# Two layers of cross attention on one core: queries of two units projected together in every second slot

## The chip, the cores and the metric

The kernel runs on one core of a Trainium2 chip. The metric is device time in microseconds (us) of one execution. The core has four compute engines that run their own instruction streams and meet only at semaphores: PE (TensorE, matrix products into the accumulation banks), ACT (ScalarE), DVE (VectorE) and POOL (GpSimd). SP issues the DMA transfers in this kernel, one after another, and each issue takes SP's time.

## The reference

There are 32 batches of x [112, 512], a context [375, 512] and an additive mask [112, 375], which is zero in these inputs. Two layers follow each other, each of this form (32 query heads of 16, 8 key and value heads, groups of 4):

```python
q = x @ Wq + bq;  k = ctx @ Wk + bk;  v = ctx @ Wv + bv
scores = einsum('bkgld,bksd->bkgls', q, k) * scale + mask
attn = softmax(scores);  out = einsum('bkgls,bksd->bkgld', attn, v)
x = layernorm(out @ Wo + bo + x) * gamma + beta
```

All of it is float32 on the outside. The context is the same for both layers.

## The kernel before, in words

A unit is one batch in one layer: 64 units, in two parities p = 0 and 1 (batch 2n + p is unit n of parity p). The program is a row of slots, (0, i), (1, i), (0, i + 1) and so on, and each engine's stream is written out by hand slot by slot in `run`, with a loop over i in the middle of each layer. In slot (p, i) five units are worked on (`units`, L57): `main` has its scores, exps and weighted values made; `ahead`, of the other parity o, gets its values projected and its row maxima; `post`, of parity o, gets its second half of weighted values and its output projection; `proj`, of parity p, gets keys and queries projected; `stored`, of parity p, gets its residual, layer norm and store.

A slot has 12 pieces. In each, PE makes two score products `sc` (L746, 448 columns), and around them stands other work. `maximum` (L754) makes a pair of products `ms` whose row maxima DVE takes; 16 pairs a slot, spread over the pieces by `PAIRS_AT`. `values` (L767) multiplies probabilities and values into the bank `pv`, 12 products for half a unit. `max_columns` (L788) turns the maxima, as negated bf16 parts, into `job`; ACT casts them to `mT`, and a DMA puts them as rows into `qs`, so that the score product subtracts the maximum. `project_values` (L795), `project_keys` (L806), `project_outputs` (L817), `transpose_rows` (L830, layer 0 only) and `project_queries` (L840) are float32 products.

There are eight banks: two for `sc`, four for `ms`, one `pv` (values, keys, turned rows) and one `job` (projected values, queries, outputs, turned maxima). Each user of `job` first waits until the last one has been emptied (`take_job_bank`, L732).

Queries: PE fills `job` with four heads of 112 columns (L846, 16 products), ACT adds the bias and scales into `qf` (L565), and the float32 is split into three bf16 parts `qp` (ACT L570 and L579, POOL L483 and L491). Keys go the same way into `kp`. SP then copies the parts into stacked operands `qs` and `ks` by small transfers (`stack_terms`, L301): 6 terms for each of q and k and for each half of the heads, 24 a slot. The first half (h = 0) is issued at the end of a slot, the second at the start of the next. SP's other transfers in a slot are two rows of `mT` (L310), four of `oraw` (L315, L316), the mask (L270), the context (L265), the turned x (`xT`, L278), x (L288), the result y (L294) and in layer 0 its turned form (L299). Scores cannot start before the `mT` row has landed (L750), nor the maxima of a half before its stack has (L756).

Of the kernel before, what the change touches and what calls it, by code (L numbers as in the profile page):

```python
# [8 lines left out]
ALU = mybir.AluOpType  # L9
ACT = mybir.ActivationFunctionType  # L10
# [10 lines left out]
KC = 3  # L21
# [79 lines left out]
def cross_attention_two_layers(nc, xT_d, x_d, ctxT_d, mask_d, mflat_d, W, out):  # L101
# [4 lines left out]
    with ExitStack() as ctx:  # L106
# [40 lines left out]
        xT = two(sb, "xT", [P, DC, S])  # L147
# [3 lines left out]
        qf = sb("qf", [P, GL])  # L151
# [57 lines left out]
        q_ps = two(sem, "q_ps")  # L209
# [4 lines left out]
        q_evac = two(sem, "q_evac")  # L214
# [39 lines left out]
        def _(sp):  # L254
# [17 lines left out]
            def load_xT(p, n, layer):  # L272
                b, before = batch(p, n, layer), count(n)
                turned = count(16 * (n - PER) + 16) if layer == 1 else 0
                need(sp, q_ps[p], before)
                need(sp, yT_out[p], turned)
                src = xT_d if layer == 0 else yT_d
                sp.dma_start(xT[p][:, :, :].rearrange("p a b -> p (a b)"), src[b]).then_inc(xT_in[p], 16)  # L278
# [39 lines left out]
            def slot(p, i, has, lay):  # L318
# [19 lines left out]
                if m_ok:  # L338
                    max_rows(p, 1, count(2 * main + 2))
                if s_ok:  # L340
                    store_y(p, stored, lay[4])
                if more and not (isinstance(ahead, int) and ahead + 1 == 0):
                    after = lay[3] if not isinstance(ahead, int) else 0 if ahead + 1 < PER else 1
                    load_ctx(o, ahead + 1, after)
                    load_xT(o, ahead + 1, after)
                if m_ok:
                    load_x(p, main, lay[0])
                if j_ok:
                    sp.wait_ge(k_p3[p], keys)
                    stack_terms(p, 0, ks[p], kp[p], 1)  # L350
                    sp.wait_ge(q_p1[p], queries)
                    stack_terms(p, 0, qs[p], qp, 0, of=(0,))
                if m_ok:
# [46 lines left out]
            load_xT(0, 0, 0)  # L400
            for n in range(BLOADS):
# [3 lines left out]
            load_xT(1, 0, 0)  # L405
# [7 lines left out]
        def _(pool):  # L413
# [15 lines left out]
            def slot(p, i, has, lay):  # L429
# [30 lines left out]
                if m_ok:  # L460
                    max_parts(p, 1, main, (p, 2 * main + 1))
                if s_ok:
                    pool.wait_ge(ln[p], 3 * (stored + 1))
                    nc.gpsimd.tensor_tensor(rstd[:, :], veps[:, :], neghalf[:, :], ALU.pow).then_inc(rs_ready[p], 1)
                if p_ok:
                    pool.wait_ge(x_in[o], 16 * (post + 1))
                    if s_ok:
                        pool.wait_ge(o_evac[p], stored + 1)
                    nc.gpsimd.tensor_tensor(res[:, :], xin[o][:, :], bo[lay[2]][:, :], ALU.add).then_inc(res_ready[o], 1)
                if j_ok:  # L470
# [4 lines left out]
                if p_ok:  # L475
                    weighted(0)
                if a_ok:
                    max_parts(o, 0, ahead, (p, 2 * main + 2) if m_ok else None)
                if j_ok:
                    for h in range(2):  # L480
                        cols = slice(GL // 2 * h, GL // 2 * (h + 1))
                        pool.wait_ge(q_p1[p], 2 * proj + h + 1)
                        nc.gpsimd.tensor_tensor(qr[:, cols], qf[:, cols], qp[:, 0, cols], ALU.subtract)\  # L483
                          .then_inc(q_r[p], 1)
                if p_ok:
                    weighted(1)
                if j_ok:
                    for h in range(2):
# [3 lines left out]
                          .then_inc(q_p3[p], 1)  # L492

# [4 lines left out]
        def _(act):  # L498
            def slot(p, i, has, lay):
# [31 lines left out]

                for k in range(PIECES):
# [3 lines left out]
                    if k == 4 and j_ok:  # L536
                        act.wait_ge(k_ps[p], proj + 1)
                        if a_ok:
                            act.wait_ge(k_r[o], ahead + 1)
                        if m_ok:  # L540
                            act.wait_ge(stack[p][0], 16 * NSTACK * (main + 1))
                            act.wait_ge(stack[p][1], 16 * NSTACK * (main + 1))
                        nc.scalar.activation(kf[:, :], pv[:, 0:S2], ACT.Identity, bias=bk[lay[3]][:, 0:1])\
                          .then_inc(k_evac[p], 1)
                        act.wait_ge(k_evac[p], proj + 1)
                        nc.scalar.copy(kp[p][:, 0, :], kf[:, :]).then_inc(k_p1[p], 1)  # L546
                    if k == 3 and m_ok:
                        m_out(p, 1, main, (p, main + 1))
                    if k == 5 and j_ok:
                        act.wait_ge(k_r[p], proj + 1)  # L550
                        nc.scalar.copy(kp[p][:, 1, :], kr[:, :]).then_inc(k_p2[p], 1)
                    if k == 6 and s_ok and lay[4] == 0:
                        act.wait_ge(t_ps[p], stored + 1)
                        if not isinstance(stored, int) or 2 * stored + p > 0:
                            need(act, yT_out[o], 16 * (stored + p))
# [418 lines left out]
```

## Time and profile before

| what | value |
|---|---|
| time, median of 3 runs | 1839.72 us (1838.92 to 1845.19) |
| the profiled execution | 1841.82 us |
| its span, first to last instruction | 1839.7 us |
| mean granted TensorE clock | 0.986 |
| busy share of PE, DVE, ACT, POOL | 97%, 74%, 59%, 31% |
| chain that ended last, PE's share | 88% |

Spans and starts are microseconds from the first instruction. A line of the timeline is a run of equal instructions. An f32 product stands as two records, so 8 products are x16. The ends of PE records are modelled and overlap the next record's start, so a distance from start to start tells PE's time better than the busy time. A granted clock of 1.00 is the 2.4 GHz level.

### The profile page before, as it was taken

How to read it: one execution, taken by the hardware profiler on the slowest of the kernel's cores; microseconds unless marked ns; L12 is line 12 of the kernel's file. 1: busy time of each engine (PE TensorE's matmuls, PEld its weight loads, DVE VectorE, ACT ScalarE, POOL GpSimd, SP SyncE). 2: the span in 40 equal slices, each digit the busy share in tenths (PEclk: the TensorE clock that was granted, in tenths of full speed). 3: DMA queues.
4: the chain of work that ended last, by engine and by line, in shares of the span. 5: the costliest groups of instructions: out<-in, count | busy, mean ns of one | idle time of the engine just before them, and what ended most of it. 6: DMA issues, size and time to landing. Idle time of an engine off the chain costs nothing.

```text
span 1839.7 us, 37410 instructions
## 1 busy us (share of the span) xinstructions
PE 1778.8 (97%) x11521; PEld 1148.1 (62%) x11521; DVE 1369.8 (74%) x1808; ACT 1079.1 (59%) x2530; POOL 573.1 (31%) x1165
## 2 busy tenths in 40 slices
PE   4899899999999999999999999999999999999996
PEld 3566566666666666666666666666666666666652
DVE  6577677777777777777777777777787777777784
ACT  1465556656656656656656656656655656656653
POOL 1232223323323323323323323323323333333321
PEclk8899999999999999999999999999999999999998
DMA  9235434434434434434434434434434434443421
GB/s 287 88 124 171 139 115 143 132 116 142 133 116 142 132 118 142 132 117 142 133 120 142 127 111 131 128 107 134 130 109 132 128 114 128 128 126 116 126 85 42
DMA packets 200894, 235.92 MB, mean 128 GB/s; under 512 B 41706, under 2 KB 176100, under 8 KB 199812
## 3 DMA queue, kind: packets, MB, share of 16 engines
q1 hardware_dynamic: 200836, 235.19, 41.6%
q8 instruction: 31, 0.51, 0.1%
q14 instruction: 27, 0.22, 0.0%
HBM read 101.39 MB, written 22.02 MB: 67 GB/s over the span
## 4 chain that ended last, share of the span: by engine, by line
PE 88%; SPq 5%; DMA 2%; issue 2%; ACT 1%; POOL 1%; DVE 0%; ACTq 0%; POOLq 0%; DVEq 0%
PE ms L763 17%; PE pv L782 16%; PE sc L746 14%; PE job L824 12%; PE job L846 11%; PE job L800 9%; PE pv L812 9%; SPq L305 4%; DMA qs<-qp 1%; PE pv L837 1%; DMA qs<-mT 1%; PE job L791 0%; DMA bq<-in_bq 0%; POOL kp L474 0%; POOL kr L472 0%
## 5 line engine op out<-in xcount | busy, mean ns | idle before, releaser
L632 DVE TENSOR_REDUCE mx<-ms 112x2 f32<-112x750 f32 x1024 | 933.4, 933 | 414.7 <-PE ms L763 402.8
L516 ACT ACTIVATE probs<-sc 125x448 f32<-125x448 f32 x1536 | 751.9, 542 | 345.3 <-PE sc L746 338.1
L763 PE MATMUL ms<-ks,qs 96*112 96x375 bf16 x2048 | 500.7, 326 | 14.1 <-DMA qs<-qp 11.8
L746 PE MATMUL sc<-qs,ks 99*125 99x448 bf16 x1536 | 422.2, 355 | 13.6 <-DMA qs<-mT 11.2
L763 PEld LDWEIGHTS ms<-ks,qs 96*112 96x112 bf16 x2048 | 252.9, 130 | 230.4 <-issue 116.4
L782 PE MATMUL pv<-probs,vs 125*32 125x448 f32 x3072 | 319.1, 549 | 0.0
L746 PEld LDWEIGHTS sc<-qs,ks 99*125 99x125 bf16 x1536 | 198.5, 137 | 129.7 <-ACT probs L516 74.7
L824 PE MATMUL job<-wo,on 128*112 128x512 f32 x512 | 268.6, 606 | 7.3 <-POOL on L458 5.7
L846 PE MATMUL job<-xT,wq 128*128 128x112 f32 x2048 | 248.8, 275 | 0.0
L846 PEld LDWEIGHTS job<-xT,wq 128*128 128x128 f32 x2048 | 244.2, 192 | 3.4 <-issue 0.3
L472 POOL TENSOR_TENSOR kr<-kf,kp 128x375 f32<-128x375 f32 x64 | 57.8, 903 | 537.4 <-ACT kp L546 537.4
L647 DVE RECIPROCAL orec<-osum 128x112 f32<-128x112 f32 x256 | 214.9, 841 | 10.3 <-DMA osum<-oraw 10.3
L812 PE MATMUL pv<-ctxT,wk 128*128 128x375 f32 x512 | 184.9, 483 | 10.4 <-DMA bq<-in_bq 10.4
L800 PE MATMUL job<-wv,ctxT 128*125 128x128 f32 x1536 | 190.8, 274 | 0.0
L782 PEld LDWEIGHTS pv<-probs,vs 125*32 125x32 f32 x3072 | 87.3, 110 | 164.2 <-issue 163.4
L800 PEld LDWEIGHTS job<-wv,ctxT 128*125 128x125 f32 x1536 | 186.5, 189 | 4.1
L524 ACT COPY oraw<-pv 128x448 f32<-128x448 f32 x128 | 68.1, 532 | 171.7 <-PE pv L782 171.7
L812 PEld LDWEIGHTS pv<-ctxT,wk 128*128 128x128 f32 x512 | 96.0, 191 | 49.7 <-issue 12.1
L565 ACT ACTIVATE qf<-job,bqs 128x112 f32<-128x112 f32 x256 | 69.8, 355 | 88.0 <-PE job L846 88.0
L444 POOL TENSOR_TENSOR mwide<-mx,zero 112x16 bf16<-112x16 f32 x128 | 27.6, 215 | 278.8 <-DVE mx L632 271.2
L491 POOL TENSOR_TENSOR qp<-qr,qp 128x224 bf16<-128x224 f32 x128 | 75.4, 610 | 104.7 <-ACT qp L579 104.7
L824 PEld LDWEIGHTS job<-wo,on 128*112 128x112 f32 x512 | 82.6, 177 | 37.4 <-issue 17.7
(54 smaller groups left out, 1000.4 us busy)
## 6 DMA issues: line engine op xcount, KB each, us to landing
ctxT<-in_ctxT SPq DMA_DIRECT2D x64, 750.0 KB, 5.9
qs<-qp SPq DMA_DIRECT2D x768, 56.0 KB, 2.4
ks<-kp SPq DMA_DIRECT2D x768, 46.9 KB, 2.6
osum<-oraw SPq DMA_DIRECT2D x128, 112.0 KB, 2.6
oc<-oraw SPq DMA_DIRECT2D x128, 112.0 KB, 2.6
mask<-in_mask SPq DMA_DIRECT2D x64, 164.1 KB, 2.3
xT<-in_xT SPq DMA_DIRECT2D x32, 224.0 KB, 6.6
xin<-in_x SPq DMA_DIRECT2D x32, 224.0 KB, 6.7
```

What stands on the lines that cost most here:

```text
L305: sp.dma_start(dst[HD * t:HD * t + HD, 4 * h:4 * h + 4, :].rearrange("d g n -> d (g n)"), src[64 * h:64 * h + 64, parts[which], :]).then_i ...
L491: nc.gpsimd.tensor_tensor(qp[:, 2, cols], qr[:, cols], qp[:, 1, cols], ALU.subtract)\
L516: nc.scalar.activation(probs[0:KCS, k, j, :], sc[j][0:KCS, 0:GL], ACT.Exp)\
L632: nc.vector.tensor_reduce(mx[o][:, 2 * j:2 * j + 2], ms[j % 2][0:S, :, 0:S2], AX_X, ALU.max)\
L647: nc.vector.reciprocal(orec[:, S * n:S * n + S], osum[:, S * n:S * n + S])\
L746: last = nc.tensor.matmul(sc[j][0:KCS, 0:GL], ks[p][0:KM, g, rows], qs[p][0:KM, g, :], start=True, stop=not masked)
L763: last = nc.tensor.matmul(ms[j % 2][0:S, n, 0:S2], qs[o][0:KT, g, S * c:S * c + S], ks[o][0:KT, g, :], start=True, stop=True)
L782: last = nc.tensor.matmul(pv[32 * j:32 * j + 32, 0:GL], vs[u][:, chunk, 4 * h + j, :, :].rearrange("s d two -> s (d two)"), probs[0:KCS, H ...
L800: last = nc.tensor.matmul(job[0:KCS, P * c:P * c + P], ctxT[o][:, t, KCS * c:KCS * c + KCS], wv[lay[1]][:, t, :], start=(t == 0), stop=(t ...
L812: last = nc.tensor.matmul(pv[:, 0:S2], wk[lay[3]][:, t, :], ctxT[p][:, t, :], start=(t == 0), stop=(t == DC - 1))
L824: last = nc.tensor.matmul(job[0:S, 0:D], on[:, S * c:S * c + S], wo[lay[2]][:, c, :], start=(c == 0), stop=(c == NG - 1))
L846: last = nc.tensor.matmul(job[:, S * c:S * c + S], wq[lay[3]][:, t, c, :], xT[p][:, t, :], start=(t == 0), stop=(t == DC - 1))
```

## The change

The queries of both units of one index (parities 0 and 1) are projected in slot (0, i), each product over 224 columns (`xT` holds both units side by side), and slot (1, i) has no query products. The four heads no longer fit in `job` at once: heads 0 and 1 fill its 448 columns, ACT moves them to `qf` (now for two units), then come heads 2 and 3. Slot (1, i) still splits its own unit's queries out of `qf`.

The output projection of the post unit of parity 1 is divided: heads 0 and 1 stay in slot (0, i), at pieces 10 and 11, and heads 2 and 3 come in pieces 0 and 1 of slot (1, i) (`LATE_HEADS_AT`). The places of all other PE steps, of the ACT, DVE and POOL steps that answer them, and of SP's transfers are now written per parity.

```diff
-PAIRS_AT = [2, 2, 1, 2, 0, 1, 1, 1, 2, 2, 1, 1]
+PAIRS_AT = [[1, 1, 1, 1, 1, 1, 1, 2, 1, 2, 2, 2], [1, 1, 1, 1, 2, 1, 1, 1, 2, 2, 2, 1]]
+LATE_HEADS_AT = [{}, {0: (2,), 1: (3,)}]
+HEADS_AT = [{10: (0,), 11: (1,)}, {8: (0,), 9: (1,), 10: (2,), 11: (3,)}]
+KEYS_AT = [{2: (0,), 3: (1, 2), 4: (3,)}, {2: (0, 1), 3: (2, 3)}]
+VALUES_AT = [{1: (0, 1), 2: (2,)}, {4: (0, 1), 5: (2,)}]
+QUERIES_AT = [{4: (0,), 5: (1,), 6: (2,), 7: (3,)}, {}]
+COLUMNS_AT = [(9, 3), (7, 2)]
+TURNED_AT = [6, 6]
+FIRST_HALF_AT = [8, 7]
+QUERY_PARTS_AT = [7, 4]
+RESIDUAL_AT = [0, 1]
+ROWS_AT = [4, 3]
...
-        xT = two(sb, "xT", [P, DC, S])
+        xT = sb("xT", [P, DC, PAR, S])
-        qf = sb("qf", [P, GL])
+        qf = sb("qf", [P, PAR, GL])
...
+                if p == 1 and (not isinstance(proj, int) or 0 < proj + 1 < UNITS):
+                    after = lay[3] if not isinstance(proj, int) else 0 if proj + 1 < PER else 1
+                    for u in range(PAR):
+                        load_xT(u, proj + 1, after)
...
+                def q_out(heads):
+                    act.wait_ge(q_ps, 2 * proj + heads[-1] // 2 + 1)
+                    if heads[0] == 0:
+                        for u in range(PAR):
+                            need(act, q_r[u], 2 * proj)
+                    for c in heads:
+                        nc.scalar.activation(qf[:, :, S * c:S * c + S],
+                                             job[:, PAR * S * (c % 2):PAR * S * (c % 2 + 1)].rearrange("p (u l) -> p u l", u=PAR),
+                                             ACT.Identity, bias=bqs[lay[3]][:, c:c + 1], scale=SCALE).then_inc(q_evac, 1)
...
                     def project_queries(heads):
+                        if heads[0] % 2 == 0:
+                            take_job_bank()
                         if 0 in heads:
-                            take_job_bank()
-                            pe.wait_ge(xT_in[p], 16 * (proj + 1))
+                            for u in range(PAR):
+                                pe.wait_ge(xT_in[u], 16 * (proj + 1))
                         for c in heads:
                             for t in range(DC):
-                                last = nc.tensor.matmul(job[:, S * c:S * c + S], wq[lay[3]][:, t, c, :], xT[p][:, t, :],
+                                last = nc.tensor.matmul(job[:, PAR * S * (c % 2):PAR * S * (c % 2 + 1)], wq[lay[3]][:, t, c, :],
+                                                        xT[:, t, :, :].rearrange("p u l -> p (u l)"),
                                                         start=(t == 0), stop=(t == DC - 1))
-                        if NG - 1 in heads:
-                            last.then_inc(q_ps[p], 1)
-                            job_free[0] = (q_evac[p], NG * (proj + 1))
+                        if heads[-1] % 2 == 1:
+                            last.then_inc(q_ps, 1)
+                            job_free[0] = (q_evac, NG * proj + heads[-1] + 1)
...
-                        next_maximum()
+                        if k > 0 or p == 0:
+                            next_maximum()
+                        if k in LATE_HEADS_AT[p] and s_ok:
+                            project_outputs(p, stored, lay[4], LATE_HEADS_AT[p][k])
```

PE, from piece 5 of a slot on, before (any parity; `sc` scores, `ms` a maxima pair, `job<-xT,wq` queries, `pv<-ident,y` turned rows, `pv<-probs,vs` weighted values):

```order
L763 MATMUL ms<-ks,qs 112x375 x2
L846 MATMUL job<-xT,wq 128x112 x8
L746 MATMUL sc<-qs,ks 125x448 x2
L763 MATMUL ms<-ks,qs 112x375 x2
L837 MATMUL pv<-ident,y 128x112 x4
L846 MATMUL job<-xT,wq 128x112 x8
L746 MATMUL sc<-qs,ks 125x448 x2
L763 MATMUL ms<-ks,qs 112x375 x2
L782 MATMUL pv<-probs,vs 32x448 x12
```

The same engine in the slot of parity 0 now, from piece 4 on:

```order
L921 MATMUL job<-xT,wq 128x224 x4
L818 MATMUL sc<-qs,ks 125x448 x2
L835 MATMUL ms<-ks,qs 112x375 x2
L921 MATMUL job<-xT,wq 128x224 x4
L818 MATMUL sc<-qs,ks 125x448 x2
L835 MATMUL ms<-ks,qs 112x375 x2
L909 MATMUL pv<-ident,y 128x112 x4
L921 MATMUL job<-xT,wq 128x224 x4
L818 MATMUL sc<-qs,ks 125x448 x2
L835 MATMUL ms<-ks,qs 112x375 x2
L921 MATMUL job<-xT,wq 128x224 x4
```

Two groups of two heads have become four of one head with twice the columns, one piece earlier, and the third needs the bank of the first two.

PE behind the first-half values, before (`job<-negident,mwide` turned maxima, `job<-wo,on` an output head):

```order
L782 MATMUL pv<-probs,vs 32x448 x12
L791 MATMUL job<-negident,mwide 128x112
L746 MATMUL sc<-qs,ks 125x448 x2
L763 MATMUL ms<-ks,qs 112x375 x2
L824 MATMUL job<-wo,on 112x512
L763 MATMUL ms<-ks,qs 112x375 x2
```

The same place in the slot of parity 0 now:

```order
L854 MATMUL pv<-probs,vs 32x448 x12
L818 MATMUL sc<-qs,ks 125x448 x2
L835 MATMUL ms<-ks,qs 112x375 x2
L863 MATMUL job<-negident,mwide 128x112
L835 MATMUL ms<-ks,qs 112x375 x2
L818 MATMUL sc<-qs,ks 125x448 x2
L835 MATMUL ms<-ks,qs 112x375 x2
L896 MATMUL job<-wo,on 112x512
```

The turned maxima stand behind a scores pair, and the first output head comes one piece later.

SP from the loads of x to the end of a slot, before (`ks<-kp` and `qs<-qp` stacked parts, `qs<-mT` the maxima rows):

```order
L265 DMA ctxT<-in_ctxT 128x1500
L278 DMA xT<-in_xT 128x448
L288 DMA xin<-in_x 112x512
L305 DMA ks<-kp 16x4x375 x6
L305 DMA qs<-qp 16x4x448 x3
L315 DMA osum<-oraw 64x448
L316 DMA oc<-oraw 64x448
L310 DMA qs<-mT 3x16x112
L305 DMA qs<-qp 16x4x448 x3
```

The same stretch in the slot of parity 1 now, in layer 1:

```order
L296 DMA xT<-yT_mid 128x4x112 x2
L306 DMA xin<-in_x 112x512
L323 DMA ks<-kp 16x4x375 x6
L283 DMA ctxT<-in_ctxT 128x1500
L323 DMA qs<-qp 16x4x448 x5
L328 DMA qs<-mT 3x16x112
L333 DMA osum<-oraw 64x448
L334 DMA oc<-oraw 64x448
L323 DMA qs<-qp 16x4x448
```

The context load stands behind the keys, both `xT` loads ahead of them, and only the last query part is left at the end.

## Rows read from the trace of the kernel before

**Rows 1.** The page: busy time and share of each engine.

```profile
PE 1778.8 (97%) x11521; PEld 1148.1 (62%) x11521; DVE 1369.8 (74%) x1808; ACT 1079.1 (59%) x2530; POOL 573.1 (31%) x1165
```

**Rows 2.** Table by stage: window, length, busy PE, PEld, DVE, ACT, POOL, clock, DMA.

```profile
550.00:715.00 165.00, 164.79 (x1091) 107.63 (x1090) 125.36 (x169) 101.69 (x239) 53.36 (x108) 1.00 0.42 131
1210.00:1375.00 165.00, 164.80 (x1078) 106.94 (x1077) 127.66 (x171) 100.48 (x237) 53.41 (x108) 1.00 0.40 123
```

**Rows 3.** Timeline of PE, layer 0: start, length, line, operation.

```profile
806.18 2.46 PE L782 MATMUL pv<-probs,vs 125*32 125x448 f32 x24
...
820.04 1.91 PE L800 MATMUL job<-wv,ctxT 128*125 128x128 f32 x16
821.79 0.48 PE L763 MATMUL ms<-ks,qs 96*112 96x375 bf16 x2
...
825.77 2.06 PE L812 MATMUL pv<-ctxT,wk 128*128 128x375 f32 x6
827.67 0.54 PE L746 MATMUL sc<-qs,ks 99*125 99x448 bf16 x2
828.05 0.48 PE L763 MATMUL ms<-ks,qs 96*112 96x375 bf16 x2
828.37 1.94 PE L846 MATMUL job<-xT,wq 128*128 128x112 f32 x16
830.14 0.55 PE L746 MATMUL sc<-qs,ks 99*125 99x448 bf16 x2
...
833.01 0.54 PE L746 MATMUL sc<-qs,ks 99*125 99x448 bf16 x2
...
833.81 2.46 PE L782 MATMUL pv<-probs,vs 125*32 125x448 f32 x24
836.20 0.22 PE L791 MATMUL job<-negident,mwide 112*128 112x112 bf16 x1
...
836.65 0.48 PE L763 MATMUL ms<-ks,qs 96*112 96x375 bf16 x2
837.19 1.11 PE L824 MATMUL job<-wo,on 128*112 128x512 f32 x2
838.14 0.49 PE L763 MATMUL ms<-ks,qs 96*112 96x375 bf16 x2
...
841.04 1.02 PE L824 MATMUL job<-wo,on 128*112 128x512 f32 x2
841.90 0.54 PE L746 MATMUL sc<-qs,ks 99*125 99x448 bf16 x2
```

**Rows 4.** Timeline of PE, layer 1: the second-half values of two slots.

```profile
1229.59 2.46 PE L782 MATMUL pv<-probs,vs 125*32 125x448 f32 x24
...
1256.81 2.46 PE L782 MATMUL pv<-probs,vs 125*32 125x448 f32 x24
```

**Rows 5.** Timeline of ACT, the same slot of layer 0.

```profile
833.42 1.09 ACT L565 ACTIVATE qf<-job,bqs 128x112 f32<-128x112 f32 x4 [1.39 <-PE job L846]
...
836.47 0.53 ACT L524 COPY oraw<-pv 128x448 f32<-128x448 f32 x1 [0.53 <-PE pv L782]
836.89 0.24 ACT L530 CAST mT<-job 48x112 bf16<-48x112 f32 x1
837.04 0.97 ACT L516 ACTIVATE probs<-sc 125x448 f32<-125x448 f32 x2
```

**Rows 6.** Timeline of DVE, the same slot.

```profile
838.66 3.66 DVE L632 TENSOR_REDUCE mx<-ms 112x2 f32<-112x750 f32 x4 [0.55 <-PE ms L763]
```

**Rows 7.** Timeline of SP's issues, the same slot.

```profile
831.51 3.78 SPq L305 DMA_DIRECT2D ks<-kp  x6
...
838.52 0.81 SPq L310 DMA_DIRECT2D qs<-mT  x1
839.38 1.90 SPq L305 DMA_DIRECT2D qs<-qp  x3
```

**Rows 8.** The chain that ended last, near the start: a transfer from issue to landing.

```profile
56.09 2.30 DMA qs<-qp
```

More of the change, by code:

```diff
@@ L49 @@
 PAIRS = NH // 2
-PAIRS_AT = [2, 2, 1, 2, 0, 1, 1, 1, 2, 2, 1, 1]
-PAIR0 = [sum(PAIRS_AT[:k]) for k in range(PIECES + 1)]
+PAIRS_AT = [[1, 1, 1, 1, 1, 1, 1, 2, 1, 2, 2, 2], [1, 1, 1, 1, 2, 1, 1, 1, 2, 2, 2, 1]]
+PAIR0 = [[sum(at[:k]) for k in range(PIECES + 1)] for at in PAIRS_AT]
 HH = NH // 2
 NSTACK = 2 * NT
-assert KCS * KC == S2 and PAIR0[-1] == PAIRS and KM <= P and PAIR0[7] >= PAIRS // 2
+LATE_HEADS_AT = [{}, {0: (2,), 1: (3,)}]
[9 more added lines that the diff above has]
+ROWS_AT = [4, 3]
+RECIPROCALS_AT = [4, 4]
+KEYS_END = [max(at) for at in KEYS_AT]
+VALUES_END = [max(at) for at in VALUES_AT]
+assert KCS * KC == S2 and KM <= P and all(at[-1] == PAIRS and at[n[0]] >= PAIRS // 2 for at, n in zip(PAIR0, COLUMNS_AT))
 def units(p, i):
@@ L208, in cross_attention_two_layers @@
         v_ps = two(sem, "v_ps")
-        q_ps = two(sem, "q_ps")
+        q_ps = sem("q_ps")
         o_ps = two(sem, "o_ps")
@@ L213, in cross_attention_two_layers @@
         k_evac = two(sem, "k_evac")
-        q_evac = two(sem, "q_evac")
+        q_evac = sem("q_evac")
         k_p1 = two(sem, "k_p1")
@@ L350, in slot @@
                     stack_terms(p, 0, ks[p], kp[p], 1)
+                if more and p == 1 and not (isinstance(ahead, int) and ahead + 1 == 0):
+                    load_ctx(o, ahead + 1, lay[3] if not isinstance(ahead, int) else 0 if ahead + 1 < PER else 1)
+                if j_ok:
                     sp.wait_ge(q_p1[p], queries)
                     stack_terms(p, 0, qs[p], qp, 0, of=(0,))
+                    if p == 1:
+                        sp.wait_ge(q_p2[p], queries)
+                        stack_terms(p, 0, qs[p], qp, 0, of=(1,))
+                if a_ok and p == 1:
+                    max_rows(o, 0, count(2 * ahead + 1))
                 if m_ok:
@@ L400, in _ @@
             load_xT(0, 0, 0)
+            load_xT(1, 0, 0)
             for n in range(BLOADS):
@@ L535, in slot @@
                         pv_out(o, 1, post, post + o)
[L536 to L549, printed above, removed]
+                    if k == KEYS_END[p] + 1 and j_ok:
                         act.wait_ge(k_r[p], proj + 1)
                         nc.scalar.copy(kp[p][:, 1, :], kr[:, :]).then_inc(k_p2[p], 1)
[L552 to L555, printed above, removed]
-                        nc.scalar.copy(yT[:, :, :].rearrange("p a b -> p (a b)"), pv[:, 0:GL])\
-                          .then_inc(yT_ready[p], 1)
-                    if k == 6 and j_ok:
-                        act.wait_ge(q_ps[p], proj + 1)
+                    if k == COLUMNS_AT[p][1] and m_ok:
+                        m_out(p, 1, main, (p, main + 1))
+                    if k == KEYS_END[p] and j_ok:
+                        k_out()
+                    if k == TURNED_AT[p] and s_ok and lay[4] == 0:
+                        rows_out()
+                    if k in QUERIES_AT[p] and QUERIES_AT[p][k][-1] % 2 == 1 and j_ok:
+                        q_out((QUERIES_AT[p][k][-1] - 1, QUERIES_AT[p][k][-1]))
+                    if k == QUERY_PARTS_AT[p] and j_ok:
                         if a_ok:
```

189 lines of the change are left out of this document (109 added, 80 removed).

## The prediction

> **What bounds the kernel now.** I read the page's busy shares, then a table by stage, then the PE timeline of one slot, then ACT, DVE and SP beside it. PE is busy for 97% of the span, DVE for 74% [rows 1]. In the steady stretches of both layers PE is busy for 164.8 of 165 us at a granted clock of 1.00 (the 2.4 GHz level) [rows 2], so a saving counts only if it shortens PE's stream or its waits. The profiler spreads busy time over short waits, so I take start-to-start distances. From the second `pv` group of one slot to that of the next it is 27.63 us in layer 0 (806.18 to 833.81 [rows 3]) and 27.22 in layer 1 [rows 4]. A pair of slots is thus 55.26 and 54.44 us. The profiled execution took 1841.82 us for a span of 1839.7; the median shown is 1839.72, so a change of the span carries over one to one.
>
> **Pitches.** All from [rows 3]. An f32 product is two records. 16 records of 112 columns (L846) take 830.14 − 828.37 = 1.77 us, 0.1106 each. 16 of 128 columns (L800) take 1.75, 0.1094 each. Six of 375 (L812) take 1.90, 0.3167 each. Two of 512 (L824) take 0.86, 0.430 each. So 112 columns cost no less than 128: below that width something other than columns sets the pace, the 128-column weight load. A scores pair is 0.38 and a maxima pair 0.32.
>
> **Query products.** Per pair of slots 64 records of 112 columns become 32 of 224. The nearest rows bound a record of 224 between 0.109 (128 columns) and 0.317 (375). The line through them gives 0.1094 + 96 × 0.00084 = 0.190, and at 512 it gives 0.432 against the measured 0.430, so I hold 0.190 to within 0.005. Removed 64 × 0.1106 = 7.08, added 32 × 0.190 = 6.08: −1.00 us per pair. At the bounds it would be −3.6 or +3.1, which I leave out of the range because of the fit at 512.
>
> A sentence by itself: the Trainium skill (TensorE: Matmul & The Clock Gate, "Back-to-back issue gap") gives a sustained spacing of 81 ns at 128 columns and 131 at 512, so wide products would be nearly free, and by an estimate from that the pair would save some 4 us. Here a bf16 product of 375 columns has half of 0.32, 160 ns, and the f32 row grows linearly with columns, so the trace disagrees and decides.
>
> **The first query evacuation.** Two units do not fit in one bank: heads 0 and 1 fill `job` (448 columns), and heads 2 and 3 must wait until ACT has emptied it (`take_job_bank` on `q_evac`). Before, all four heads had their own columns and no wait. After a query group ends (833.01, the next scores) `qf` starts 0.41 us later [rows 3, 5]. Four of 112 columns take 1.09, 0.27 each, and two of 448 take 0.97, 0.49 each [rows 5]; 224 columns lie at 0.34, so two need about 0.75 with the tail. The bank is free 0.41 + 0.75 + 0.04 = 1.20 us after head 1 ends. Between head 1 and head 2 stand a scores pair and a maxima pair, 0.70, and in layer 0 the turning of rows, 0.39. PE waits 0.50 in layer 1 and 0.11 in layer 0, and pays a weight load that is not hidden: the first output product after such a wait takes 0.95 against 0.86 [rows 3], +0.09. Together +0.59 and +0.20. Ends: 0, if ACT is quicker by all of it, and 1.20, if nothing covers it.
>
> A rule speaks against this edit, in a sentence by itself: the Trainium skill (Perfetto Trace Analysis, "Matmuls") says that independent groups should rotate through PSUM banks so that the evacuation of one overlaps the next. The trace agrees where it can: the output product at 837.19 starts just as the `mT` cast ends (836.89 + 0.24) [rows 3, 5].
>
> **After the first-half values.** In the slot of parity 0, `values` moves from piece 7 to 8 and `max_columns` to piece 9, behind the scores. ACT's `oraw` starts 0.27 after `pv` ends (836.20 to 836.47), the next operation 0.42 later, and an exp takes 0.54, a pair 0.97 [rows 5]. So the first exp of piece 9 ends 1.23 after `pv`, the second 1.67. PE reaches the scores of piece 10 after 0.38 + 0.32 + 0.06 + 0.32 = 1.08, must wait to 1.29 for the first bank and to 1.73 for the second, and is then 0.46 late. In return the first output product has no wait any more (before: 837.19 − 836.65 − 0.32 = 0.22, and the 0.09): −0.31. Ends for the +0.46: 0 and 0.7.
>
> **Parity 1.** Slot 1 loses all queries and gets the last two output heads, laid out 25.4 us in layer 1 (25.8 in layer 0); slot 0 becomes 28.8. Its first maxima pair comes only after `values`, 3.7 us into the slot, which leaves 21.7 us. DVE is busy 125.36 of 165 us, that is 21.0 per slot of 27.63 [rows 2]. Of this two maxima of 0.92 (four in 3.66 [rows 6]) may end in the next slot, so DVE keeps up, with 2 to 3 us in hand at the end and, where maxima come in twos in pieces 8 to 10, a few tenths. POOL's split of the first eight maxima ends about when `pv` does. I take +0.10 for all of it; ends 0 and 0.6.
>
> **SP's queue.** A stack transfer costs SP 0.63 (six in 3.78), an `mT` row 0.81 [rows 7], and a landing comes 2.30 after the issue, 2.9 from its start [rows 8]. Moved past in slot 1: both `xT` loads ahead of the keys, the `ctxT` load behind them, the middle query part and `mT` ahead of the outputs. The keys' last part is there 831.51 − 827.67 = 3.84 after their product [rows 3, 7]; that product ends 9.6 us into slot 1, so keys start at 13.5. Behind them 6 + 5 transfers, one load, one `mT` and two outputs end at 22.9, and the last query part lands at 25.8. PE wants it for the first maxima of slot 0, at 25.4 + 0.38. That cover is nearly nothing in layer 1, 0.5 in layer 0. In slot 0 `mT` starts at about 25.5 and lands near 28, with 0.8 to spare. Nothing added to the sum here, up to +1 per pair in the range.
>
> **The sum.** Layer 1: −1.00 − 0.31 + 0.59 + 0.46 + 0.10 = −0.16 per pair. Layer 0: −0.55. With 16 pairs of layer 0 and 15 of layer 1: −8.8 − 2.4 = −11.2 us. At the start the second slot projects keys ahead of values (2.6 us of PE earlier, 24 records of 0.109) and no queries, while the first slot has twice the query work behind SP's keys: −1.5 (−3 to +2). At the end the last slot of parity 0 sheds two output products of 0.86 while the next has room on PE: −1. Together −13.7: a span of 1826.0, and a median of 1826.0 us.
>
> **The rivals.**
> 1. No new waits: ACT empties the bank in time, or PE's waits only replace slack. Then the 1.00 stays whole: −31 − 2.5 = −33.5, 1806 us (with the freed output wait of 0.31 as well it could be 1797). For it: the 1.00 is PE work that disappears whatever the queues do. Against it: the latencies of [rows 5].
> 2. The waits eat it all: the bank wait of layer 1 in both layers (+0.39 × 16 = 6) and DVE or POOL late at parity 1 (+0.3 × 31 = 9): 1841 us, no change.
> 3. Slower: SP's queue decides. The last query part has no cover at the start of slot 0. Each 0.1 us by which the keys' parts or one of SP's own waits come later goes into PE's wait before the first maxima of slot 0. From 0.45 us per pair on the gain is gone; at 0.9 us it is +28 − 13.7: 1854 us. For it: SP issues 9.4 us without a pause behind the keys. Against it: the slot of parity 1 has slack before the keys' parts are ready.
> 4. The change does not do what it says: the 224 columns cost as much as two products of 112 (0.221). Then the 1.00 is gone: +31, 1857 us. Against it stands the line through three widths.
>
> **Chances.** The forecast 0.42 (1814 to 1836), rival 1 0.26, rival 2 0.17, rival 3 0.12, rival 4 0.03. Range 1804 to 1844: it leaves out the far end of rival 1 and most of rivals 3 and 4. A difference under 0.5% (9.2 us) is what a measurement of this kernel cannot tell from none. Faster by more than that (below 1830.5): 0.75 of the forecast's case and all of rival 1, 0.58. Within: 0.27. Slower: rivals 3 and 4, 0.15.
>
> **What would show it.** Right: query groups of 8 records at 1.52 us; a gap of 1.2 us between the end of head 1 and the weight load of head 2; scores of piece 10 that wait for exp behind `oraw`; slots of about 28.8 and 25.5 us. Wrong: PE waiting for `qs<-qp` at the start of parity 0 (rival 3), maxima waiting for DVE in pieces 8 to 11 of parity 1 (rival 2), or no wait ahead of head 2 (rival 1).

## The result: 0.23% faster, less than half of the forecast

| | before | after |
|---|---|---|
| time, median of 20 runs each | 1842.12 us (1836.52 to 1845.5) | 1837.86 us (1834.49 to 1841.65) |
| ratio of times, 95% interval | | 0.9977 (0.9969 to 0.9985) |
| span of the profiled execution | 1839.7 us | 1833.1 us |
| mean granted clock | 0.986 | 0.986 |

The gain is 4.3 us by the medians, where the prediction said 13.7. The time lies inside the range (1804 to 1844), but the gain is nearer to rival 2 ("the waits eat it all", 1841) than to the forecast. The prediction held that a difference under 0.5% cannot be told from none; with 20 executions on each side it can, and the interval leaves out 1. One execution of e9 (2280 us, granted clock 0.75) and one of e12 (1884 us, 0.94) further down ran at a lowered clock and stand in no time or ratio.

The page of the changed kernel answers to [rows 1]:

```profile
PE 1772.7 (97%) x10497; PEld 1105.6 (60%) x10497; DVE 1356.2 (74%) x1808; ACT 1049.3 (57%) x2402; POOL 589.4 (32%) x1165
```

PE has 1024 records fewer: 2048 of 112 columns became 1024 of 224. PE's busy time falls by only 6.1 us. The table by stage, the view of [rows 2], gives for a window in each layer (length, busy PE, PEld, DVE, ACT, POOL, clock, DMA):

```profile
465.00:630.00 165.00, 164.64 (x1001) 105.05 (x1000) 125.14 (x169) 99.34 (x228) 55.07 (x108) 1.00 0.44 132
...
1185.00:1350.00 165.00, 163.56 (x980) 101.59 (x972) 124.95 (x168) 96.95 (x222) 55.29 (x109) 1.00 0.42 123
```

PE is still the engine that is never free and the granted clock is the same 1.00, so the answer is in the stream of PE. The measure used from here on is the length of a **pair of slots**, from one second-half `pv` group to the one four groups later. It repeats to 0.02 us through most of a layer, and the tables give that value. A few pairs are longer, by up to 1.4 us, and in both kernels the two that start near 155 and 170 us are longer by 9 to 10 us: there SP issues the loads of layer 1's weights, and PE waits once for the maxima row (`qs<-mT`), 7.97 us before and 6.39 after. The time of a single execution scatters by some 4 us.

| | layer 0 | layer 1 |
|---|---|---|
| pair before (forecast took 55.26 and 54.44) | 55.30 | 54.50 |
| pair after | 54.83 | 54.83 |
| difference measured | −0.47 | +0.33 |
| difference forecast | −0.55 | −0.16 |

With 16 and 15 pairs this is −7.5 + 5.0 = −2.5 us. The start brought −3.0 (the first `pv` group of the steady stretch starts at 129.44 instead of 132.43), the longer pairs, the seam of the layers and the end the other −1.1 of the 6.6 by which the span fell. Not all of the −3.0 need belong to the change: the mean granted clock from 60 us to that group was 0.96 before and 1.00 after, and in the experiments e5 and e4, which leave the start nearly as it is, the same group starts at 127.68 and 131.67. The pairs do not hang on this. Layer 0 became faster and layer 1 slower.

**PE's timeline after, layer 1, slot of parity 0** (start, length, line, operation, records; in brackets the idle time that the profile sees before it). It answers to [rows 3]:

```profile
1228.36 1.68 PE L921 MATMUL job<-xT,wq 128*128 128x224 f32 x8
1229.87 0.54 PE L818 MATMUL sc<-qs,ks 99*125 99x448 bf16 x2
...
1232.47 0.48 PE L835 MATMUL ms<-ks,qs 96*112 96x375 bf16 x2
1233.12 1.78 PE L921 MATMUL job<-xT,wq 128*128 128x224 f32 x8 [0.17 <-ACT qf L614]
1234.74 0.54 PE L818 MATMUL sc<-qs,ks 99*125 99x448 bf16 x2
...
1238.07 2.46 PE L854 MATMUL pv<-probs,vs 125*32 125x448 f32 x24
1240.46 0.59 PE L818 MATMUL sc<-qs,ks 99*125 99x448 bf16 x2
...
1241.27 0.48 PE L835 MATMUL ms<-ks,qs 96*112 96x375 bf16 x2
1241.63 0.84 PE L818 MATMUL sc<-qs,ks 99*125 99x448 bf16 x2
1242.41 0.53 PE L835 MATMUL ms<-ks,qs 96*112 96x375 bf16 x2
1242.78 1.02 PE L896 MATMUL job<-wo,on 128*112 128x512 f32 x2
```

Eight records of 224 columns take 1229.87 − 1228.36 = 1.51 us: 0.189 each, as forecast. Ahead of head 2 the maxima start at 1232.47 and take 0.32, the product starts at 1233.12, and the group takes 1.62 instead of 1.51: 0.33 + 0.11 = 0.44 us for the bank. The scores of piece 10 take 1242.41 − 1241.63 = 0.78 instead of 0.38, and with the small gaps of 0.04 and 0.05 ahead of them and behind the next maxima it is about 0.48. The output product follows the maxima by 0.37, where it took 0.54 before [rows 3].

**The slot of parity 1 after, layer 1, and ACT beside it**, the place that the prediction passed over:

```profile
1258.95 1.04 PE L872 MATMUL job<-wv,ctxT 128*125 128x128 f32 x8
1259.82 0.54 PE L818 MATMUL sc<-qs,ks 99*125 99x448 bf16 x2
1260.20 0.48 PE L835 MATMUL ms<-ks,qs 96*112 96x375 bf16 x2
1260.87 0.84 PE L818 MATMUL sc<-qs,ks 99*125 99x448 bf16 x2 [0.18 <-ACT probs L579]
1261.54 0.48 PE L835 MATMUL ms<-ks,qs 96*112 96x375 bf16 x2
```

```profile
1260.27 0.98 ACT L579 ACTIVATE probs<-sc 125x448 f32<-125x448 f32 x2 [0.54 <-PE sc L818]
```

The scores of pieces 6 (1259.82) and 7 (1260.87) have one maxima pair between them, 0.70 us of work for PE. The first exp starts 0.45 after its scores and takes 0.54, and PE starts 0.06 after that, 1.05 after piece 6 began: it waits 0.35. The second exp ends 0.44 later, so the second product is late as well: the two take 0.67 instead of 0.38, +0.29. Together +0.64 us. ACT had been idle for 0.54 before that exp. This is a turnaround PE, ACT, PE, not a busy ACT. Before, a group of query products of 1.77 us stood between these two scores, which were 833.01 − 830.14 = 2.87 us apart [rows 3]. In layer 0 the turned rows (0.38) stand there now, and the same place costs less:

```profile
655.51 0.55 PE L909 MATMUL pv<-ident,y 112*128 112x112 f32 x4
655.89 0.80 PE L818 MATMUL sc<-qs,ks 99*125 99x448 bf16 x2
656.53 0.48 PE L835 MATMUL ms<-ks,qs 96*112 96x375 bf16 x2
```

0.64 − 0.38 = +0.26, and no wait before it. Turned rows fill this gap and the one ahead of head 2, which is why both layers have the same pair although layer 0 has 0.76 more to do.

The lengths of the slots, counted from the first scores of each, show that parity 1 is where the forecast missed (layer 1):

```profile
1217.11 0.54 PE L818 MATMUL sc<-qs,ks 99*125 99x448 bf16 x2
...
1245.84 0.54 PE L818 MATMUL sc<-qs,ks 99*125 99x448 bf16 x2
...
1271.94 0.54 PE L818 MATMUL sc<-qs,ks 99*125 99x448 bf16 x2
```

The slot of parity 0 takes 28.73 us (forecast 28.8), that of parity 1 takes 26.10 (forecast 25.5).

**SP's issues after, slot of parity 1**, the view of [rows 7]:

```profile
1257.79 1.48 SPq L296 DMA_DIRECT2D xT<-yT_mid  x2
...
1259.98 3.84 SPq L323 DMA_DIRECT2D ks<-kp  x6
...
1264.50 3.10 SPq L323 DMA_DIRECT2D qs<-qp  x5
...
1269.84 0.62 SPq L323 DMA_DIRECT2D qs<-qp  x1
```

The last query stack is issued at 1269.84. The maxima that need it start at 1272.32, 2.48 later and with no wait. Where PE did wait for this stack, in e6 and e8 below, it started 2.46 and 2.42 after the issue began (1270.88 to 1273.34, 1274.48 to 1276.90). So the cover is about nothing, as forecast, and it does not bind yet.

### The profile page after: what moved, and what is told of

It reads as the page before. It is cut to its first block and busy times, and to the rows that moved or that the text cites. A ratio compares the mean times of both kernels' runs of the same rounds, so it can differ in the third digit from the quotient of the medians.

```text
span 1833.1 us, 35282 instructions
## 1 busy us (share of the span) xinstructions
PE 1772.7 (97%) x10497; PEld 1105.6 (60%) x10497; DVE 1356.2 (74%) x1808; ACT 1049.3 (57%) x2402; POOL 589.4 (32%) x1165
## 2 busy tenths in 40 slices
DMA packets 225469, 235.89 MB, mean 129 GB/s; under 512 B 74475, under 2 KB 200677, under 8 KB 224389
## 5 line engine op out<-in xcount | busy, mean ns | idle before, releaser
L818 PE MATMUL sc<-qs,ks 99*125 99x448 bf16 x1536 | 442.1, 361 | 14.6 <-DMA qs<-mT 8.5
L818 PEld LDWEIGHTS sc<-qs,ks 99*125 99x125 bf16 x1536 | 194.0, 137 | 179.0 <-issue 75.7
L921 PE MATMUL job<-xT,wq 128*128 128x224 f32 x1024 | 217.4, 355 | 3.5 <-ACT qf L614 3.5
L884 PE MATMUL pv<-ctxT,wk 128*128 128x375 f32 x512 | 191.7, 487 | 10.6 <-DMA bq<-in_bq 10.6
L921 PEld LDWEIGHTS job<-xT,wq 128*128 128x128 f32 x1024 | 189.8, 190 | 19.6 <-ACT qf L614 9.1
L492 POOL TENSOR_TENSOR kr<-kf,kp 128x375 f32<-128x375 f32 x64 | 72.8, 1137 | 345.5 <-ACT kp L605 345.5
L512 POOL TENSOR_TENSOR rstd<-veps,neghalf 112x1 f32<-112x1 f32 x64 | 36.5, 570 | 253.5 <-DVE veps L743 253.5
```

The costliest lines, as they stand in the source:

```text
L492: nc.gpsimd.tensor_tensor(kr[:, :], kf[:, :], kp[p][:, 0, :], ALU.subtract).then_inc(k_r[p], 1)
L818: last = nc.tensor.matmul(sc[j][0:KCS, 0:GL], ks[p][0:KM, g, rows], qs[p][0:KM, g, :], start=True, stop=not masked)
L884: last = nc.tensor.matmul(pv[:, 0:S2], wk[lay[3]][:, t, :], ctxT[p][:, t, :], start=(t == 0), stop=(t == DC - 1))
L921: last = nc.tensor.matmul(job[:, PAR * S * (c % 2):PAR * S * (c % 2 + 1)], wq[lay[3]][:, t, c, :], xT[:, t, :, :].rearrange("p u l -> p (u ...
```

## The experiments

Theory A: the time is in turnarounds. Where two score pairs of neighbouring pieces have too little between them, PE waits for the exps. Theory B: ACT is late as a whole at parity 1 (a backlog of casts). Theory C: SP's queue is the next bound. "Pair" is the pair of slots; `+` lines are the experiment's, `-` lines those of the changed kernel. Experiments with one execution have no interval; their single times scatter by as much as the effects, so they are judged by pairs. A ratio is the measured one with its interval and can differ by 0.001 from the quotient of the medians; the kernel before had medians of 1841.9 to 1843.5 us beside e8 to e12.

| kernel | pair, layer 0 | pair, layer 1 | time, us | ratio to before |
|---|---|---|---|---|
| changed kernel | 54.83 | 54.83 | 1837.86 | 0.9977 |
| e1 values spread | 55.37 | 54.88 | 1842.73 (one execution) | |
| e2 two of 112 | 55.86 | 55.86 | 1863.83 (one execution) | |
| e3 maxima ahead of head 2 | 54.79 | 54.51 | 1830.87 (one execution) | |
| e4 exps first | 54.83 | 54.83 | 1843.26 (one execution) | |
| e5 casts later | 54.84 | 54.84 | 1833.03 (one execution) | |
| e6 spread and casts | 54.89 | 54.80 | 1835.89 (one execution) | |
| e7 parity 0 anew | 54.86 | 54.27 | 1833.30 (one execution) | |
| e8 both parities | 54.85 | 54.26 | 1834.46 | 0.9961 (0.9948 to 0.9973) |
| e9 both, queue relieved | 54.57 | 53.69 | 1817.59 | 0.9872 (0.9851 to 0.9893) |
| e10 queue relieved alone | 54.83 | 54.83 | 1836.00 | 0.9971 (0.9962 to 0.9981) |
| e11 parity 0, queue relieved | 54.52 | 54.12 | 1821.98 | 0.9891 (0.9874 to 0.9907) |
| e12 parity 1, queue relieved | 54.90 | 54.41 | 1831.60 | 0.9941 (0.9922 to 0.9961) |

### e1: something between pieces 6 and 7

```diff
-VALUES_AT = [{1: (0, 1), 2: (2,)}, {4: (0, 1), 5: (2,)}]
+VALUES_AT = [{1: (0, 1), 2: (2,)}, {4: (0,), 5: (1,), 6: (2,)}]
```

> The changed kernel, with the three value chunks of the parity 1 slot in pieces 4, 5 and 6 (one each) and not 4, 4, 5. The changed kernel's pairs of slots are 54.83 us in both layers. Theory A (turnaround): in pieces 6 and 7 of parity 1 only a maxima pair (in layer 0 also the turning) stands between two scores pairs, and PE waits for the exps of the one before, 0.64 us in layer 1 and 0.26 in layer 0; with 0.87 us of values between them the wait goes: pairs of 54.2 and 54.57. Theory B (ACT late from the query splits of parity 1): the wait only moves to another piece, pairs stay within 0.1 of 54.83. Theory C (SP's queue has no cover at the start of parity 0): layer 1 gains under 0.3 us, since the first maxima of the next slot then wait for the last query part.

The wait of piece 7 went, and the pair did not fall (54.88; layer 0 rose by 0.54). PE, and ACT beside it:

```profile
1263.83 0.74 PE L818 MATMUL sc<-qs,ks 99*125 99x448 bf16 x2
1264.41 0.49 PE L835 MATMUL ms<-ks,qs 96*112 96x375 bf16 x2
1264.73 1.04 PE L872 MATMUL job<-wv,ctxT 128*125 128x128 f32 x8
1265.90 0.75 PE L818 MATMUL sc<-qs,ks 99*125 99x448 bf16 x2
1266.48 0.48 PE L835 MATMUL ms<-ks,qs 96*112 96x375 bf16 x2
```

```profile
1263.15 0.97 ACT L579 ACTIVATE probs<-sc 125x448 f32<-125x448 f32 x2
1264.25 0.50 ACT L631 CAST kp<-kr 128x375 bf16<-128x375 f32 x1
1264.66 0.65 ACT L648 CAST qp<-qf 128x224 bf16<-128x224 f32 x2
1265.22 0.97 ACT L579 ACTIVATE probs<-sc 125x448 f32<-125x448 f32 x2
```

Pieces 5 and 6 now come before ACT has got through its key and query casts: scores take 0.58 twice (+0.20 each), and 1.17 lie between 1264.73 and 1265.90 for a product of 0.87 (+0.30). Here theory B applies: work moved out of piece 4 brings the next scores forward onto a busy ACT. One hole was closed and another opened, so the price of the first stayed hidden.

### e2: the width undone

```diff
-                                last = nc.tensor.matmul(job[:, PAR * S * (c % 2):PAR * S * (c % 2 + 1)], wq[lay[3]][:, t, c, :],
-                                                        xT[:, t, :, :].rearrange("p u l -> p (u l)"),
-                                                        start=(t == 0), stop=(t == DC - 1))
+                                pass
+                            for u in range(PAR):
+                                for t in range(DC):
+                                    at = PAR * S * (c % 2) + S * u
+                                    last = nc.tensor.matmul(job[:, at:at + S], wq[lay[3]][:, t, c, :], xT[:, t, u, :],
+                                                            start=(t == 0), stop=(t == DC - 1))
```

> The changed kernel, with each 224-column query product made as two of 112, one per unit, everything else as it is. If a record of 224 columns costs 0.190 us and one of 112 0.1106, PE gets 64 x 0.1106 - 32 x 0.190 = 1.00 us more per pair: 55.8 us in both layers, about +31 us in all. If the saving is hidden behind other engines' waits in part, less: under +0.5 per pair. The wait for the query bank should stay the same, about 0.4 us in layer 1.

+1.03 us per pair in both layers. The line of this group on the two pages (busy, mean of one record) shows the records, after first, e2 behind:

```profile
L921 PE MATMUL job<-xT,wq 128*128 128x224 f32 x1024 | 217.4, 355 | 3.5 <-ACT qf L614 3.5
```

```profile
L925 PE MATMUL job<-xT,wq 128*128 128x112 f32 x2048 | 250.5, 276 | 3.5 <-ACT qf L614 3.5
```

The 33.1 us of busy time between them are 1.03 for each of 32 indices. The term of the width was right.

### e3: two maxima ahead of head 2

The two added lines stand behind the first `next_maximum()` of a piece, ahead of the products.

```diff
-PAIRS_AT = [[1, 1, 1, 1, 1, 1, 1, 2, 1, 2, 2, 2], [1, 1, 1, 1, 2, 1, 1, 1, 2, 2, 2, 1]]
+PAIRS_AT = [[1, 1, 1, 1, 1, 1, 2, 1, 1, 2, 2, 2], [1, 1, 1, 1, 2, 1, 1, 1, 2, 2, 2, 1]]
...
+                        if k == 6 and p == 0:
+                            next_maximum()
```

> The changed kernel, with two maxima pairs ahead of query head 2 in piece 6 of parity 0 (and one pair fewer in piece 7). If the wait ahead of head 2 (0.33 us and a weight load not hidden, 0.10, layer 1) is the bank's evacuation, 0.32 us more of cover takes nearly all of it: pairs of 54.4 to 54.5 in layer 1, 54.75 to 54.83 in layer 0. If it is something else that ends at a fixed time before the next scores, nothing: 54.83.

Layer 1 fell by 0.32, layer 0 by 0.04: a second maxima pair of 0.32 replaces the wait of 0.33, and in layer 0 there was next to none to replace. What is left is the weight load that is not hidden (1.62 for the group instead of 1.51). The bank was the cause of this wait.

### e4: exps ahead of the copy of `oraw`

In the slot of parity 0 ACT empties `pv` behind the exps of piece 9 instead of ahead of them, and SP sends the `mT` row ahead of the outputs.

```diff
-                    if k == FIRST_HALF_AT[p] and m_ok:
+                    if p == 1 and k == FIRST_HALF_AT[p] and m_ok:
...
+                    if p == 0 and k == FIRST_HALF_AT[p] + 1 and m_ok:
+                        pv_out(p, 0, main, main + p if p_ok else None)
```

> The changed kernel, with ACT in parity 0 taking the exps of piece 9 and the turned maxima ahead of the copy of the first-half values, and SP issuing the maxima row ahead of those outputs. If the wait of the piece 10 scores (0.44 us) comes from the copy standing ahead of the exps, it falls to about 0.15 and the pair by 0.2 to 0.3 us in both layers (54.55 to 54.6), unless the first output head then waits for the later maxima (up to 0.2 of it given back). If the wait is the turnaround of exps alone, under 0.1.

The expected 0.2 to 0.3 did not come: no change. PE's weight loads show why (e4, layer 1):

```profile
1249.16 0.13 PEld L818 LDWEIGHTS sc<-qs,ks 99*125 99x125 bf16 x1 [0.30 <-ACT probs L577]
1249.64 0.18 PEld L835 LDWEIGHTS ms<-ks,qs 96*112 96x112 bf16 x2 [0.34 <-DVE mx L710]
```

The first score product of piece 10 no longer waits, the second and the maxima behind it do, and the maxima wait for DVE. Two maxima pairs stand close together on either side of the turned maxima, and DVE takes 0.92 for each. Two waits of nearly equal length lay one behind the other, and taking one away brings nothing. (SP's order was changed in the same edit; it shows in no wait of PE here.)

### e5 and e6: the casts of parity 1 a piece later, alone and with e1

```diff
-QUERY_PARTS_AT = [7, 4]
+QUERY_PARTS_AT = [7, 5]
```

> The changed kernel (pairs 54.83 us), with parity 1's query casts on ACT in pieces 5 and 7 and not 4 and 6. The spread values of the first experiment showed waits in front of the scores of pieces 5 and 6 that came from ACT's queue (keys and query casts back to back). If the wait in front of the scores of piece 7 in the changed kernel (0.64 us in layer 1, 0.26 in layer 0) is also ACT's backlog, it shrinks by 0.3 us or more; if it is the turnaround of one scores pair alone (scores, exp, next scores with 0.70 us between), it stays: 54.83, within 0.05.

> Parity 1 with both edits: values chunks in pieces 4, 5 and 6, and query casts in pieces 5 and 7. If turnaround and backlog are the two causes and nothing else binds there, both waits are gone: 54.2 us in layer 1 and 54.57 in layer 0. If SP's queue has no cover (theory C), layer 1 stops at 54.5 or above and PE waits for the last query part at the start of parity 0.

e5 alone changed nothing (54.84), and the wait of piece 7 stands with a less busy ACT:

```profile
1256.98 0.84 PE L818 MATMUL sc<-qs,ks 99*125 99x448 bf16 x2 [0.18 <-ACT probs L579]
1257.65 0.48 PE L835 MATMUL ms<-ks,qs 96*112 96x375 bf16 x2
```

So the wait of piece 7 is theory A, and B falls as its cause. In e6 that wait is gone, 0.20 is left at piece 5, and yet the pair is 54.80. The place where the rest went:

```profile
1258.39 0.75 PE L818 MATMUL sc<-qs,ks 99*125 99x448 bf16 x2
1258.98 0.48 PE L835 MATMUL ms<-ks,qs 96*112 96x375 bf16 x2
...
1272.54 0.54 PE L818 MATMUL sc<-qs,ks 99*125 99x448 bf16 x2
1273.34 0.52 PE L835 MATMUL ms<-ks,qs 96*112 96x375 bf16 x2 [0.26 <-DMA qs<-qp]
```

At the start of parity 0 PE now waits 0.42 for the last query stack. A slot on PE that is 0.4 shorter meets a queue of SP that is not.

### e7 and e8: parity 0 laid anew, alone and with e6

All query heads come a piece later, the first-half values behind them, two maxima ahead of head 2, and SP sends the `mT` row ahead of the outputs. e8 has `QUERY_PARTS_AT = [8, 5]` and the edit of e1 besides.

```diff
-QUERIES_AT = [{4: (0,), 5: (1,), 6: (2,), 7: (3,)}, {}]
+QUERIES_AT = [{5: (0,), 6: (1,), 7: (2,), 8: (3,)}, {}]
...
-TURNED_AT = [6, 6]
-FIRST_HALF_AT = [8, 7]
-QUERY_PARTS_AT = [7, 4]
+TURNED_AT = [7, 6]
+FIRST_HALF_AT = [9, 7]
+QUERY_PARTS_AT = [8, 4]
...
-                if a_ok and p == 1:
+                if a_ok:
...
+                        if k == 7 and p == 0:
+                            next_maximum()
```

> The changed kernel, with parity 0 laid out again: queries in pieces 5 to 8, two maxima pairs (and the turned rows) ahead of head 2, first-half values in piece 9 right ahead of the turned maxima, so that the output head waits 0.31 us as in the kernel before, and the maxima row ahead of the outputs in SP's queue. The bank wait (0.43, layer 1) and the wait behind the values (0.44 to 0.48, both layers) go, 0.31 comes: 54.2 to 54.3 in layer 1, 54.6 to 54.7 in layer 0. If DVE's pace of maxima or a late maxima row binds, at most half of that.

> Both parities laid out again, the last two experiments together. If the gains add, pairs of 53.6 us in layer 1 and 54.4 in layer 0, against 54.50 and 55.30 in the kernel before: about 28 us, 1.5%, a ratio of 0.985. If SP's queue binds at the start of parity 0 (cover about nothing in the changed kernel), layer 1 gains at most half: a ratio of 0.989 to 0.992.

e7 brought 0.56 in layer 1, nothing in layer 0. In layer 0 the 0.48 behind the first-half values went, 0.24 came ahead of the turned rows, where four maxima products now stand together, and the rest went into a wait at the start of the next slot of parity 0, where the maxima start 2.43 us after SP began to issue the last query stack (723.62). e7, layer 0:

```profile
726.05 0.52 PE L833 MATMUL ms<-ks,qs 96*112 96x375 bf16 x2 [0.16 <-DMA qs<-qp]
```

e8 brought nothing beyond e7: the gains of the parities do not add, and its ratio of 0.9961 is worse than either branch of what was expected. Its PE at the start of parity 0, and SP ahead of it:

```profile
1275.99 0.54 PE L816 MATMUL sc<-qs,ks 99*125 99x448 bf16 x2
1276.90 0.52 PE L833 MATMUL ms<-ks,qs 96*112 96x375 bf16 x2 [0.37 <-DMA qs<-qp]
```

```profile
1207.95 1.49 SPq L296 DMA_DIRECT2D xT<-yT_mid  x2
...
1210.15 3.83 SPq L323 DMA_DIRECT2D ks<-kp  x6
```

The maxima start 0.91 after the scores instead of 0.38: PE waits 0.53, and 0.04 more behind the maxima. Two `xT` loads cost SP 1.49 us ahead of the key stacks. That is rival 3 of the prediction, now that PE's slot is short enough to meet it.

### e9 and e10: the queue relieved, with e8 and alone

The `xT` loads go from slot 1, ahead of its key stacks, to slot 0, behind its first-half key stacks. The `ctxT` load of parity 1 goes from behind the key stacks to the slot's end.

```diff
-                if p == 1 and (not isinstance(proj, int) or 0 < proj + 1 < UNITS):
-                    after = lay[3] if not isinstance(proj, int) else 0 if proj + 1 < PER else 1
-                    for u in range(PAR):
-                        load_xT(u, proj + 1, after)
...
+                if p == 0 and (not isinstance(proj, int) or 0 < proj + 1 < UNITS):
+                    after = lay[3] if not isinstance(proj, int) else 0 if proj + 1 < PER else 1
+                    for u in range(PAR):
+                        load_xT(u, proj + 1, after)
```

> As e8_both_parities, but SyncE's queue of parity 1 is shortened: the two loads of xT (0.74 us of issue each) move from slot 1 to behind the first-half key stacks of slot 0, where the queue stood idle for 2.7 us, and the load of ctxT moves behind the last query stack. Theory C (queue): in e8 TensorE waited 0.74 and about 0.4 us a pair of slots in layer 1 for qs<-qp at the start of slot 0, and about 0.3 in layer 0. The last query stack now comes some 0.9 us sooner, the waits go, and the pair falls from 54.26 to 53.3 to 53.6 in layer 1 and from 54.85 to 54.5 to 54.6 in layer 0; the time falls to 1816 to 1822 us. Theory A (turnaround): another wait for exponentials or maxima stands right behind, as it did in e4; the pair stays at 54.0 or more in layer 1.

> The changed kernel with the queue edit of e9 alone. In the changed kernel the last query stack landed 2.48 us after its issue began, just when TensorE asked for it, with no wait. Theory A (turnaround): the pair of slots is set by the waits for exponentials in piece 10 of parity 0 and piece 7 of parity 1, so this changes nothing: 54.83 and 54.83, within 0.05. Theory C (queue): the queue sets the pair in the changed kernel too, and the pair falls by 0.3 or more in layer 1.

Alone the edit changes nothing (54.83 twice), as A said. On top of e8 it brings 0.57 in layer 1 and 0.28 in layer 0. PE at the start of parity 0 in e9:

```profile
1263.03 0.54 PE L816 MATMUL sc<-qs,ks 99*125 99x448 bf16 x2
1263.40 0.48 PE L833 MATMUL ms<-ks,qs 96*112 96x375 bf16 x2
1263.82 2.46 PE L852 MATMUL pv<-probs,vs 125*32 125x448 f32 x24
```

No wait for `qs<-qp` is left. The pair is 0.09 above the upper end of what was expected in layer 1, because the expectation took e8's wait for the stack as 0.74 and some 0.4, while the rows above give 0.57: 54.26 − 0.57 = 53.69, all of it. What is left of the added waits is 0.23 ahead of head 2 and 0.20 at piece 5 of parity 1. The kernel takes 1817.59 us against 1841.99 for the one before, ratio 0.9872 (0.9851 to 0.9893), and against 1836.00 for e10, which has the pairs of the changed kernel: it beats both. The two moves of loads were not tried one by one.

### e11 and e12: each parity alone on the relieved queue

> The queue edit of e9 with parity 0 alone laid anew (the edit of e7), parity 1 as in the changed kernel. If the gains of the two parities add once the queue has cover (theory A for the sizes, C for why e8 fell short): e9 is 1.14 below the changed kernel in layer 1 (53.69 against 54.83), and the wait in piece 7 of parity 1 with what came in its place was worth 0.64 - 0.20 = 0.44, so this pair is 54.1 to 54.3 in layer 1, and its scores of piece 7 stand 0.3 behind the exponentials as before. If the queue edit itself brought what e9 gained over e8, whatever stands in parity 1 (theory C alone): 53.7 to 53.9.

> The queue edit of e9 with parity 1 alone laid anew (the edits of e6), parity 0 as in the changed kernel. e6 kept a wait of some 0.42 us for qs<-qp at the start of parity 0 and stood at 54.80 in layer 1. If the gains add: 54.83 - 0.44 = 54.4 (54.3 to 54.5) in layer 1, and the wait for the query stack is gone. If something other than the queue held e6 up: 54.7 or more.

In layer 1 parity 0 alone is worth 54.83 − 54.12 = 0.71, parity 1 alone 0.42, together 1.13. e9 has both and stands 1.14 below the changed kernel. With cover in the queue the gains add. e11 keeps the wait of piece 7, e12 the one ahead of head 2:

```profile
1253.63 0.84 PE L816 MATMUL sc<-qs,ks 99*125 99x448 bf16 x2 [0.18 <-ACT probs L577]
```

```profile
1233.58 1.78 PE L921 MATMUL job<-xT,wq 128*128 128x224 f32 x8 [0.17 <-ACT qf L614]
```

The 0.42 is the 0.64 of piece 7 less the 0.20 that comes up at piece 5. In layer 0, e12 is 0.07 above the changed kernel, since the turned rows had covered most of that gap.

## Why the prediction was wrong

The sum per pair, as forecast and as measured:

| term | forecast, layer 1 / 0 | measured, layer 1 / 0 | by |
|---|---|---|---|
| query width | −1.00 | −1.03 | e2 |
| freed wait of the first output product | −0.31 | −0.27 | before and after: 0.26 + 0.32 over the plain lengths in the two slots of a pair, now 0.31 in one |
| bank ahead of head 2 | +0.59 / +0.20 | +0.44 / +0.06 | after, e3 |
| scores of piece 10 | +0.46 | +0.48 | after, e4 |
| parity 1 | +0.10 | +0.64 / +0.26 | after, e5, e12 |
| small gaps elsewhere | | +0.06 | after |
| SP's queue | 0 | 0 | e10 |
| sum | −0.16 / −0.55 | +0.32 / −0.44 | |
| pair measured | | +0.33 / −0.47 | |

**The step that failed** is "Parity 1 … I take +0.10 for all of it; ends 0 and 0.6". It looked at DVE and POOL, neither of which costs PE anything there, and left out ACT. Taking the queries out of slot 1 was counted as work removed from PE, with the price per product, but those products were also what stood between two score pairs while ACT emptied their banks. With the prediction's own numbers the wait in piece 7 could have been worked out, as was done for piece 10 of the other parity: one score product 0.19, ACT starts 0.27 after PE ends, an exp 0.54, a pair 0.97, PE 0.06 after the exp. The second bank is free 1.49 after the scores of piece 6 begin, and PE, with 0.70 of work, wants it at 0.89: 0.60 late. Measured is 0.64 in layer 1, just above the end given, and 0.26 in layer 0. Against the +0.10 this is 0.54 × 15 + 0.16 × 16 = 10.7 us, more than the 9.4 by which the whole forecast missed.

**Point by point.** The pitch of 224 columns held to 0.001 us. The bank wait was there, a quarter smaller than worked out: the product starts 1.03 us after head 1 ends (1232.09 to 1233.12), where 1.20 was given. The wait behind the first-half values was there and of the right size; its second half is not the exps alone but DVE's maxima as well (e4), which the prediction did not see. The freed wait came, at 0.27. The start brought 3.0 instead of 1.5, part of it perhaps by the clock. SP's cover was zero and cost nothing, as said, though the parts of it were off: the `xT` loads cost twice what they had, and the last stack was there 2.4 after its issue began, not 2.9. Layer 0 came within 0.08 per pair, and that is luck in part: its parity 1 cost 0.16 more than forecast and its bank wait 0.14 less. The error of the pairs is in layer 1, 0.49 × 15 = 7.4 us, where −11.2 was forecast for both layers.

**The rivals.** Rival 1 (no new waits) is out: three waits stand in the trace. Rival 2 came nearest in size, with the wrong place: not DVE or POOL late at parity 1 and not the bank wait in layer 0, but ACT's turnaround. Rival 3 did not decide in the changed kernel (e10) and became the bound once PE's waits were taken away (e6, e8, e9). Rival 4 is out (e2).

Left open: how much of the 3.0 us at the start is the change, and the one long wait for `qs<-mT` while layer 1's weights are loaded (7.97 us before, 6.39 after, 11.58 in e9). It is worth more than all that was won in the changed kernel, and no experiment touched it.

## What to carry to other kernels

Work taken out of an engine that is always busy may have been the filler between a producer and the buffer that it needs back. Before you count its price as won, list what stands between neighbouring uses of each buffer in the new order, and compare it with the turnaround, at every piece and not only where something was added (here 1.05 us for PE, ACT, PE against 0.70 laid out). Where two waits of the same length lie one behind the other, or a queue has zero cover, an edit of one shows nothing; test the edits together, and each with the cover restored, before you call one worthless.

## What the hardware showed that was not expected

The issue of an `xT` load took SP 0.74 us (two in 1.48) where it took 0.34 before, for the same 224 KB. Before:

```profile
1242.82 0.34 SPq L278 DMA_DIRECT2D xT<-yT_mid  x1
```

The destination is now four rows of 448 bytes in each partition, every second one of a wider tile, instead of one run. The page counts 74475 packets under 512 bytes, 41706 before: 32769 more, and 64 loads of 128 partitions with four rows each are 32768. The median from issue to landing fell all the same, from 6.6 to 4.1 us (layer 0). In e10 the loads stand at another place in SP's queue and two still take 1.47 us (1236.48), so the place is not what doubled the issue; with it moved, the landing is 3.8. Before, each load stood right behind the `ctxT` load of 750 KB, in the other two kernels it does not. Whether that or the split rows made the landing shorter was not tried by itself.
